# Attention queries projected with features on the partitions, two pairs ahead, and regrouped by transfers inside SBUF

## What is computed

```
h = layernorm(x) * (1 + ca) + sa
fused = h @ w_kv_a                          # 192 | 64 | 64
q = rmsnorm(fused[:, :192]) @ w_qb          # 16 heads x (128 + 64)
kv = rmsnorm(fused[:, 192:256]) @ w_kvb     # 16 heads x (128 + 128)
q_pe, k_pe = rope(q[..., 128:]), rope(fused[:, 256:])
probs = softmax(causal(q . k / sqrt(192)));  x = x + ga * (probs @ v) @ w_o
h = layernorm(x) * (1 + cb) + sb
x = x + gb * (experts(h, top 4 of 16) + shared_ffn(h))
rope: q_pe * cos + rotate_half(q_pe) * sin
```

## Time and profile before

| | |
|---|---|
| median of 3 executions | 1230.08 us (1229.61 to 1230.75) |
| the profiled execution, its span | 1228.7 us |
| PE busy | 95% of the span |
| DVE, ACT, POOL busy | 68%, 54%, 23% |

### The profile page before, as it was taken

The page is one execution under the profiler, slowest core; times in us unless marked ns, Lnnn a source line. Parts: engine busy times, 40 slices in busy tenths (PEclk is TensorE's granted clock), DMA queues, the critical chain, the costliest instruction groups (busy, mean ns, idle before and its releaser), DMA issues.

```text
span 1228.7 us, 26041 instructions
## 1 busy us (share of the span) xinstructions
PE 1165.9 (95%) x7596; PEld 954.4 (78%) x7596; DVE 836.3 (68%) x2596; ACT 666.3 (54%) x1904; POOL 276.5 (23%) x332
## 2 busy tenths in 40 slices
PE   6799999999999999999999999999999999998792
PEld 3688878887788878887788779887788778886561
DVE  3577758776677668776777568776777668764541
ACT  2477635774477635774467626773467636672130
POOL 1000032221322132121312022211312122212364
PEclk8899999999999999999999999999999999999897
DMA  9520002000010001000010001000110001000793
GB/s 296 154 62 0 0 4 67 0 0 0 17 51 0 0 17 51 0 0 0 17 51 0 0 17 51 0 0 0 33 36 0 0 17 34 1 1 18 228 234 38
DMA packets 48157, 46.01 MB, mean 37 GB/s; under 512 B 10050, under 2 KB 44800, under 8 KB 48136
## 3 DMA queue, kind: packets, MB, share of 16 engines
q1 hardware_dynamic: 29096, 30.90, 8.5%
q0 software_dynamic: 7168, 6.20, 2.7%
q10 hardware_dynamic: 11872, 8.65, 2.5%
HBM read 35.04 MB, written 15.11 MB: 41 GB/s over the span
## 4 chain that ended last, share of the span: by engine, by line
PE 86%; DVE 4%; ACT 2%; POOL 2%; DMA 2%; SPq 1%; issue 1%; ACTq 1%; POOLq 0%; DVEq 0%
PE PS L691 11%; PE PS L712 11%; PE PS L830 8%; PE PS L670 7%; PE PS L671 6%; PE PS L672 6%; PE PS L656 4%; PE PS L838 4%; PE PS L859 3%; PE PS L643 3%; PE PS L646 3%; PE PS L647 3%; PE PS L644 2%; PE PS L645 2%; PE PS L809 2%; PE PS L701 2%
## 5 line engine op out<-in xcount | busy, mean ns | idle before, releaser
L1031 ACT ACTIVATE probs<-probs,nmax 128x512 f32<-128x512 f32 (+3 forms) x512 | 283.5, 555 | 167.6 <-DVE nmax L1275 164.1
L1275 DVE CUSTOM_DVE_ANT_0 probs<-PS,cmask 128x512 f32<-128x512 f32 (+3 forms) x512 | 230.4, 488 | 117.0 <-PE PS L672 114.7
L552 POOL DMA_INDIRECT tab_dram<-entry,slot x112 | 110.5, 987 | 386.7 <-PE PS L712 365.4
L670 PE MATMUL PS<-kTh,qTh 128*128 128x512 f32 (+3 forms) x512 | 174.5, 341 | 1.5 <-DVE qTl L1306 1.5
L672 PE MATMUL PS<-kTh,qTl 128*128 128x512 f32 (+3 forms) x512 | 164.9, 322 | 0.0
L671 PE MATMUL PS<-kTl,qTh 128*128 128x512 f32 (+3 forms) x512 | 164.9, 322 | 0.0
L691 PE MATMUL PS<-ident,probs 128*128 128x128 f32 x1280 | 164.8, 275 | 0.0
L1040 ACT ACTIVATE pT<-PS 128x384 f32<-128x384 f32 (+3 forms) x320 | 124.4, 461 | 68.0 <-PE PS L691 68.0
L712 PE MATMUL PS<-pT,kmat 128*64 128x512 f32 (+3 forms) x1024 | 151.9, 439 | 0.3 <-issue 0.3
L691 PEld LDWEIGHTS PS<-ident,probs 128*128 128x128 f32 x1280 | 141.4, 140 | 10.3 <-issue 7.4
L712 PEld LDWEIGHTS PS<-pT,kmat 128*64 128x64 f32 x1024 | 68.0, 136 | 76.0 <-issue 62.1
(11 more groups left out here) (256 smaller groups left out, 2084.8 us busy)
## 6 DMA issues: line engine op xcount, KB each, us to landing
x_in<-in_x SPq DMA_DIRECT2D x8, 512.0 KB, 6.0
modb<-mod_dram SPq DMA_DIRECT2D x8, 512.0 KB, 5.4
h_dram<-mod_dram SPq DMA_DIRECT2D x1, 4096.0 KB
h_dram<-h SPq DMA_DIRECT2D x8, 512.0 KB, 3.0
out<-base SPq DMA_DIRECT2D x8, 512.0 KB, 3.5
pT<-in_wo SPq DMA_DIRECT2D x1, 2048.0 KB, 11.0
tab_dram<-entry,slot POOLq DMA_INDIRECT x112, 2.1
oT<-in_wqnT SPq DMA_DIRECT2D x1, 1536.0 KB, 11.5
```

What stands on the lines that cost most here:

```text
L552: pool.indirect_dma_start(tab_dram[:, :], bass.IndirectOffsetOnAxis(ap=slot[:, j:j + 1], axis=0), entry[:, j, :], None, bounds_check=NE * ...
L670: pe.matmul(PS[:, bank, 0:n], qTh[:, h, rows_q], kTh[:, 0:n], start=True, stop=False)
L1031: act.activation(probs[:, UO[u]:UO[u] + UW[u]], probs[:, UO[u]:UO[u] + UW[u]], ACT.Exp, scale=-1.0, bias=nmax[:, u:u + 1], accum_out=psums ...
L1275: dve.tensor_tensor_reduce(out=probs[:, UO[u]:UO[u] + UW[u]], in0=PS[:, SBANK[u], 0:UW[u]], in1=cmask[:, S - UW[u]:S], scale=-1.0, scalar= ...
```

## The change

The query is projected with its features on the partitions: 5 products of 512 columns for the latent half of both heads (`q_latent`, bank 6) and 5 for the rotary half (`q_rotary`, bank 7), so that no transposes are needed. It is done two pairs ahead; `middle` projects pairs 0 and 1. ACT and DVE split the latent half; DVE multiplies the rotary half with tables, POOL adds and takes the low part (`query_rotary`). The parts lie in `qstage` with a head's latent and rotary rows apart; six transfers for each pair on SP's queue (1 MB) bring them to `qT[p % 2]`, and unit 0 waits for them (`q_landed`). Statistics and normalisation of the next batch's input move from step 7 to step 6, its turning to the end of step 6 and the start of step 7, and output tile 0's products for pairs 0 to 5 from `middle` to step 7. The loops over pairs on PE, ACT and DVE are written out, POOL's scatters stand pair by pair among the queries, and two tables more (`cosT`, `sinT`) are loaded.

```diff
-OBANK, QBANKS = 5, [6, 7]
+OBANK, LATBANK, PEBANK = 5, 6, 7
...
+            def move(p, hl, lo, head, frm, n):
+                src = qstage[frm:frm + n, 2 * hl:2 * hl + 2, :].bitcast(F32)
+                sp.dma_start(qT[p % 2][lo:lo + n, :, head, :].bitcast(F32), src).then_inc(q_landed[p % 2], 16)
+            def move_query(b, p, fresh=False):
+                g = b * NPAIR + p
+                wait_alone(sp, latl_ready, g + 1)
+                if not fresh:
+                    wait_alone(sp, s_ps, NU * (g - 1))
+                for h in range(2):
+                    move(p, 0, 0, h, h * KL, KL)
+                wait_alone(sp, pel_ready, g + 1)
+                for h in range(2):
+                    for half in range(2):
+                        move(p, 1, KL + half * HALF, h, half * KL + h * HALF, HALF)
...
             sp.dma_start(h2_dram[0:T, H:].rearrange("(b s) h -> b s h", s=S),
                          mod_dram[:, 3 * H:].unsqueeze(1).to_broadcast([B, S, H])).then_inc(gates_out, 16)
+            for p in range(3):
+                move_query(0, p, p < 2)
             with sp.Fori(0, B - 1) as b:
                 n = b + 1
                 sp.wait_ge(h1_ready, n)
                 sp.wait_ge(res_ready, n)
                 sp.dma_start(x_in[:], rows(xr, n)).then_inc(x_landed, 16)
+                for p in range(3, NPAIR):
+                    move_query(b, p)
...
+                for p in range(2):
+                    move_query(n, p)
+                store_rows(b)
+                move_query(n, 2)
                 store_batch(b)
                 load_modb(n)
...
+            def query_rotary(g):
+                wait_alone(pool, turned_ready, g + 1)
+                pool.tensor_tensor(qr[:, 0, :], qr[:, 0, :], qr[:, 1, :], ALU.add).then_inc(rope_ready, 1)
+                wait_alone(pool, peh_ready, g + 1)
+                pool.tensor_tensor(qstage[:, 3, :], qr[:, 0, :], qstage[:, 2, :].bitcast(F32),
+                                   ALU.subtract).then_inc(pel_ready, 1)
...
+            for p in range(NPAIR):
+                query_rotary(p)
+            with pool.Fori(0, B - 1) as b:
+                n = b + 1
+                roots_pre(n)
+                roots_post(b)
+                query_rotary(n * NPAIR)
+                rows_scaled(b)
+                query_rotary(n * NPAIR + 1)
+                rows_shifted(b, n)
+                counts(b, False)
+                query_rotary(n * NPAIR + 2)
+                shared(b)
+                for p in range(1, NPAIR - 1):
+                    if p + 2 < NPAIR:
+                        query_rotary(n * NPAIR + p + 2)
+                    scatter(b, p)
+                pool.wait_ge(scattered, n * NT * TOPK * 16)
                 pool.sem_inc(entries_free, 1)
...
+            def q_project(p, bank):
+                cols = bass.ts(2 * p + (bank == PEBANK), P)
+                pe.matmul(PS[:, bank, :], wq0h[:, cols], ql0h[:], start=True, stop=False)
+                pe.matmul(PS[:, bank, :], wq0l[:, cols], ql0h[:], start=False, stop=False)
+                pe.matmul(PS[:, bank, :], wq0h[:, cols], ql0l[:], start=False, stop=False)
+                pe.matmul(PS[:, bank, :], wq1hh[:, cols], ql1s[:], start=False, stop=False)
+                pe.matmul(PS[:, bank, :], wq1l[:, cols], ql1s[:], start=False, stop=True).then_inc(q_ps, 1)
+            def q_latent(p, g, fresh=False):
+                if not fresh:
+                    pe.wait_ge(latl_ready, g)
+                q_project(p, LATBANK)
+            def q_rotary(p, g, fresh=False):
+                if not fresh:
+                    pe.wait_ge(turned_ready, g)
+                q_project(p, PEBANK)
...
-                    if i == NT - 1:
-                        pe.wait_ge(qTl_ready, 2 * g + h + 1)
+                    if u == 0:
+                        pe.wait_ge(q_landed[p % 2], landed(b, p))
...
-            def step(p, b, first, last, more):
+            def step(p, b, first, more):
                 g = b * NPAIR + p
-                if last:
+                last = p == NPAIR - 1
+                if p < NPAIR - 2:
+                    q_rotary(p + 2, g + 2)
+                elif not last:
+                    pe.wait_ge(turned_ready, (b + 1) * NPAIR)
                     pe.wait_ge(oT_ready, g)
-                    pe.wait_ge(qTl_ready, 2 * g + 2)
-                    output(1, 7, range(0, 3))
+                    output(1, PEBANK, range(0, 3))
                 else:
-                    q_project(p + 1, g + 1, (0, 1))
+                    if more:
+                        turn_h1(b + 1, 1, LATBANK)
+                    pe.wait_ge(oT_ready, g)
+                    output(1, PEBANK, (NPAIR - 3,))
                 if first and more:
                     pe.wait_ge(mid_ready, 3 * b)
                     shared_down(0)
-                scores(g, first, (3, 4))
-                if last:
-                    output(1, 7, range(3, NPAIR - 2))
-                else:
-                    q_project(p + 1, g + 1, (2, 3))
-                scores(g, first, (5, 6, 7))
+                scores(b, p, first, (3, 4))
+                if p == NPAIR - 2:
+                    output(1, PEBANK, range(3, NPAIR - 3))
+                elif last:
+                    if more:
+                        pe.wait_ge(hT_ready, 2 * (b + 2))
+                    else:
+                        pe.wait_ge(latl_ready, (b + 1) * NPAIR)
+                    output(0, LATBANK, range(0, 3))
+                scores(b, p, first, (5, 6, 7))
                 if not first:
                     values(g - 1, b)
                 if first and more:
                     shared_down(1)
                     pe.wait_ge(gated_ready, 2 * b - 1)
                 turn_probs(g, first, (0, 1))
-                if not last:
-                    q_turn(g + 1)
-                elif more:
-                    turn_h1(b + 1, 0, 6)
+                if p < NPAIR - 2:
+                    q_latent(p + 2, g + 2)
+                if last:
+                    output(0, LATBANK, range(3, NPAIR - 2))
                 turn_probs(g, first, (2, 3))
-                if last and more:
-                    turn_h1(b + 1, 1, 6)
+                if p == NPAIR - 2 and more:
+                    pe.wait_ge(latl_ready, (b + 1) * NPAIR)
+                    turn_h1(b + 1, 0, LATBANK)
                 turn_probs(g, first, (4, 5))
...
                     pe.wait_ge(oT_ready, (b + 1) * NPAIR)
-                    output(1, 7, (NPAIR - 2,))
-                    output(0, 6, range(0, NPAIR - 1))
+                    output(1, PEBANK, (NPAIR - 2,))
+                    output(0, LATBANK, (NPAIR - 2,))
                     pe.wait_ge(oT_ready, (b + 1) * NPAIR + 1)
-                    output(1, 7, (NPAIR - 1,))
-                    output(0, 6, (NPAIR - 1,)).then_inc(attn_ps, 1)
-                    output(2, 5, range(0, 2))
+                    output(1, PEBANK, (NPAIR - 1,))
+                    output(0, LATBANK, (NPAIR - 1,)).then_inc(attn_ps, 1)
+                    output(2, OBANK, range(NPAIR)).then_inc(attn_ps, 1)
...
-                    output(2, 5, range(2, NPAIR)).then_inc(attn_ps, 1)
...
-                    q_turn(n * NPAIR)
+                    q_rotary(1, n * NPAIR + 1)
+                    q_latent(1, n * NPAIR + 1)
...
+            def latent_high(b, p, fresh=False):
+                g = b * NPAIR + p
                 act.wait_ge(q_ps, 2 * g + 2)
...
+                if not fresh:
+                    act.wait_ge(q_landed[(p + 1) % 2], landed(b, p - 1) if p else landed(b - 1, NPAIR - 1))
+                act.activation(qstage[:, 0, :], PS[:, LATBANK, :], ACT.Copy).then_inc(lath_ready, 1)
+            def rotary_high(b, p):
+                act.wait_ge(rope_ready, b * NPAIR + p + 1)
+                act.activation(qstage[:, 2, :], qr[:, 0, :], ACT.Copy).then_inc(peh_ready, 1)
...
-            def step(p, b, last, more):
+            def step(p, b, more):
                 g = b * NPAIR + p
+                if p == NPAIR - 1 and more:
+                    turned_h1(b + 1, LATBANK, 1)
                 exps(g, (3, 4))
-                if not last:
-                    nope_copy(g + 1)
                 exps(g, (5, 6, 7))
                 group_out(g, 0)
                 group_out(g, 1)
-                if not last:
-                    q_high(g + 1, 0)
-                    q_high(g + 1, 1)
-                elif more:
-                    turned_h1(b + 1, (6, 6))
+                if p < NPAIR - 2:
+                    latent_high(b, p + 2)
                 group_out(g, 2)
+                if p < NPAIR - 2:
+                    rotary_high(b, p + 2)
+                elif p == NPAIR - 2 and more:
+                    turned_h1(b + 1, LATBANK, 0)
                 group_out(g, 4)
                 sums_out(g)
...
+            def q_rope(g, fresh=False):
                 def first():
...
+                    dve.wait_ge(q_ps, 2 * g + 1)
+                    if not fresh:
```

(55 more changed lines are left out.)

217 lines of the change are left out of this document (99 added, 118 removed).

## The result

The changed kernel takes 1316.03 us (median of 4, 1313.84 to 1319.27) against 1230.21 of before: a ratio of 1.0698, with an interval of 1.0669 to 1.0728. That is slower, as forecast, but by 86 us and not by 40, and outside the range that ended at 1292.

What follows compares the result with a forecast made beforehand. PE's own work, busy 95%, was taken as the bound. From 1228.7 us, prologue +20, batch 0 -1.8, batches 1 to 6 +18.6, last batch -2.9, tail -2 and clock +8 gave 1268.6, so 1270; range 1236 to 1292.

Steps and rivals of the forecast that it cites:

- Step 1: Step 1 of a batch: DVE late behind `slots`, units 6 and 7 stall 0.7 us more; 12.3 us.
- Step 6: Step 6, batches 1 to 6: root waits for the last scatter's landing, PE stalls 4.5 us before h1's turning; 16.1 us.
- Step 7: Step 7 of a batch: with output pairs and half of h1's turning added, 13.6 us against 13.05.
- the separate term of 8 for the clock: PE's lower clock after holes: 1 us for each of six stalls, 2 for holes in `middle`; +8 us (0 to 20).
- The prologue: Before the first scores: pair 0's moves wait behind the 4096 KB copy in SP's queue; +20 us (+3 to +23).
- Steady steps: Steps 2 to 5: PE's work falls by 0.85 us, unit 7 waits 0.25 for DVE; 11.6 us each against 12.20.
- `middle`: `middle` with step 0: 2.0 of the 2.6 us of output removed turns into waiting; 51.5 us against 50.56.
- The sum: Whole kernel: 1228.7 + 20 - 1.8 + 18.6 - 2.9 - 2 + 8 = 1268.6 us for the profiled execution.
- Moves that pass by: Rival, prologue: the moves pass by the copy, so the prologue costs 3 us; 1253 us, chance 0.12.
- Step 6 without a stall: Rival, step 6: POOL is done with the scatters earlier, so no stall; 1237 us, chance 0.12.
- Steady step at 12.2: Rival, steady steps: copy, move and POOL through the single `qstage` become the period; +24, about 1294 us, chance 0.10.
- The fast side: Rival, whole kernel: PE's sum holds everywhere, a batch takes 129.6 us, 1195 in all; decides at 134.4; chance 0.10.

Runs made afterwards that it cites:

- e1: The changed kernel with DVE's pairs 1 to 5 in a loop again, steps 6 and 7 written out: 1289.14 us, ratio 1.0463.
- e4: The kernel before with only DVE's loop over pairs written out: 1270.14 us, ratio 1.0324.
- e2: The changed kernel with the 16th scatter issued with pair 5's three instead of pair 6's: 1283.16 us, ratio 1.0431.
- e3: The changed kernel with the 4096 KB copy split into eight of 512 KB in SP's loop: 1295.55 us, ratio 1.0523.
- e5: The changed kernel with the edits of e1, e2 and e3 together: 1247.62 us, ratio 1.0136.
- e10: e5 with four scatters behind each of pairs 1 to 4, tile 2's residual earlier in `middle`, pair 3's moves ahead of four 512 KB transfers: 1252.85 us.
- e12: e5 with four scatters behind pairs 1 to 4, tile 2's residual earlier, latent half between units 4 and 5, gates copied before storing h2: 1202.09 us.

## Why the prediction was wrong, point by point

- **The failed step is "Step 1"**, which put 0.7 on the stall there: "DVE is late, since `slots` stands ahead of its maxima". It looked at what DVE has to do and not at where its code lies. The change writes the loops out, and the sum gave that no price. Step 1 took 18.6 for 12.3 in each of six batches, 38 us, of the 46 that the sum was short. The written-out loop is 5.3 of the 6.3, by two runs in opposite directions (e1, and e4 with 6.2 in the kernel before): PE stands 3.35 longer at unit 6 (4.71 and 1.36), and behind it works for some 3 us at the lower clock level, which costs half of that (in three of the six batches such a stretch was twice as long, and step 1 took 18.9 to 19.4 there in place of 17.9 to 18.1). In e1 the 1.36 is still 0.7 above the stall that was forecast: that is most of the 1.0 that is left, and its likely cause is an addition of DVE beside POOL (last section). For the long holes themselves, the size of the loop's body and the packets speak for code loading; how long a load takes was not measured by itself.
- **Step 6** had the right mechanism and order: PE idle 4.93 for 4.5, root directly behind the landing. The interval was 17.5 for 16.1, since PE came out of the hole at the lower clock level. Step 7 was 14.3 for 13.6 for the same reason. These 2.1 a batch, 12.6 in all, are for the most part what the separate term of 8 for the clock stood for; it was a little low, and it had nothing for step 1. The 2.9 it started from the earlier trace rows is a looser reading than it looks: that stretch at 0.50 begins at 36.60, inside the hole that ends at 38.90.
- **The prologue** was 5.6 worse than +20 (90.9 for 85). The mechanism held: without the copy ahead 19 of 25.6 came back. The first scores came at 78.7, 4 later than forecast. The rest was not taken apart.
- **Steady steps**: 11.46 for 11.6. Unit 7 is late by less than 0.25: unit 6's last product starts at 406.27 and unit 7 0.29 later instead of 0.12, so 0.17; the row names no releaser (PE's timeline):

```profile
406.27 0.29 PE L740 MATMUL PS<-kTh,qT 128*128 128x256 f32 x1
406.56 0.33 PE L738 MATMUL PS<-kTh,qT 128*128 128x128 f32 x1
```

- **`middle`**: 51.7 for 51.5, with the hole of 2.0 that was forecast ahead of h2's turning (1.98 in the row), and 1.6 more in two of seven (52.8 for 51.2), where PE ran at the lower clock level for a while:

```profile
341.23 0.88 PE L876 MATMUL PS<-ident,h 128*128 128x128 f32 x6 [1.98 <-DVE h L1312]
```

- **The sum** again, forecast and measured: prologue 20 and 25.6; batch 0 -1.8 and -3.1; batches 1 to 6 18.6 and 66.1 (11.0 each, for 3.1); steps of the last batch -2.9 and -4.0; tail -2 and +1.0; clock 8, which is in the measured rows already. That makes 39.9 forecast and 85.6 measured, 1314.3 in place of 1268.6. That the tail did not get shorter stays open; in e1, e2 and e3, whose last stage is all but the same program, it took 121.8, 117.8 and 118.4 (119.8 before), so a part of it is no more than spread.
- **The rivals.** Moves that pass by: no, 22 us held. Step 6 without a stall: no. Steady step at 12.2: no, although in e5 to e10 it was just that chain (the queue and the moves) that took back what was won elsewhere, in one step of a batch. The fast side is true of the last kernel (e12) and not of this one: with the holes gone a batch takes 132.7, under the 134.4 from which it was to decide.

What stays open: how the hole at the jump depends on the length of the body. The body of DVE's loop over batches has 525 instructions in the changed kernel and 549 in e4, with holes of 4.0 to 4.1 and 5.0 to 5.4; it has 336 in e1 and 296 in the kernel before, with an inner loop each and holes of 0.70 to 0.74 (the expectations give 437 and 260: they leave the semaphore instructions out, and by that count e1 has 288 and not 320). No length between was run, and length and inner loop were not changed apart.

## What to carry to other kernels

An engine whose loop is written out has a longer way back, and its first instructions behind the jump may come microseconds late; price it at every jump, and look for an idle time with no releaser at the top of a loop and for the packets of the instruction queue. A transfer that becomes part of the critical chain inherits everything that is issued ahead of it in its queue, so before moving work onto a queue list what stands there in each stage, and look again after each gain, since a shorter step moves the moves closer to the bulk. A hole on PE can cost more than its length, where the clock falls behind it: some 3 us here behind one of 4.9, and behind one of 2.0 in `middle` 1.6 in two batches of seven and nothing in the others.

## What was not expected of the hardware

The copy of the inverted sums on DVE (L1369, 128x512) took 426 ns before and 1192 ns after, with the same instruction. In the steady step it runs beside POOL's addition (DVE, then POOL):

```profile
409.83 1.45 DVE L1369 COPY mid<-prec 128x512 f32<-128x512 f32 x1
...
409.71 1.28 POOL L547 TENSOR_TENSOR qr<-qr 128x512 f32<-128x512 f32 x1 [2.93 <-DVE qr L1348]
```

In step 6, where POOL is idle, it took 0.43 (304.19). It begins behind POOL's addition and ends at 411.28, 0.29 after it (409.71 + 1.28 = 410.99), where its own time is 0.43. The Trainium skill (SBUF — State Buffer, section "SBUF: two separate sides") describes a pair of ports that DVE in its fast forms and GpSimd lock for a whole instruction, the other waiting; the trace agrees in the main. In the steady step DVE had the time. In step 1 it had not: there the addition of the slots ran beside POOL's addition of 2.41 and took 0.94, where it took 0.23 before, in all seven batches (DVE and POOL after, then DVE before):

```profile
375.23 0.94 DVE L1512 TENSOR_TENSOR slot_e<-slot_e,over 128x64 f32<-128x64 f32 x1
...
373.69 2.41 POOL L593 TENSOR_TENSOR base<-tmp,x 128x1024 f32<-128x1024 f32 x1
...
342.55 0.23 DVE L1429 TENSOR_TENSOR slot_e<-slot_e,over 128x64 f32<-128x64 f32 x1
```

It stands ahead of unit 3's maximum, for which PE waits at unit 6, so its 0.7 is on PE's path. No run separated either.
